# Two attention layers on one core: layer 1's output alternates between two PSUM banks

## The chip, the cores and the metric
The kernel runs on one core of one Trainium2 chip. The metric is the time of one execution on the device in microseconds (us), as the median of a few runs. The core has TensorE (PE in the profile, its weight loads PEld), VectorE (DVE), ScalarE (ACT), GpSimd (POOL) and SyncE (SP), which here only issues DMAs. Each engine works through its own queue in order; semaphores tie them together.

## The reference
The input x is (4, 256, 64, 64) in float32: 4 images of 256 channels and 4096 positions. Two attention layers follow one another.

```
# layer 0, for each image, xf = x as (256, 4096)
q = Wq @ xf + bq;  k = Wk @ xf + bk          # (32, 4096)
v = Wv @ xf + bv                             # (256, 4096)
attn = softmax(q.T @ k, axis=0)              # (4096, 4096), over i
x1   = gamma * (v @ attn) + xf
# layer 1
theta = theta_w @ x1 + theta_b               # (32, 4096)
phi   = maxpool2(phi_w @ x1 + phi_b)         # (32, 1024)
g     = maxpool2(g_w @ x1 + g_b)             # (128, 1024)
attn  = softmax(theta.T @ phi, axis=-1)      # (4096, 1024)
y     = gamma * (out_w @ (g @ attn.T) + out_b) + x1
```

## The kernel before
**Tiles and steps.** The output columns of a layer are cut into 8 chunks of 512 per image, written (l, b, n): layer, image, chunk. The summed dimension is cut into tiles of 128: 32 per chunk in layer 0, 8 in layer 1. One tile is one step g of the program. The chunks run in the order (0,0,0) to (0,0,7), then for each of three images (0,b+1,0), (1,b,0) to (1,b,7), (0,b+1,1) to (0,b+1,7), and last (1,3,0) to (1,3,7). So layer 1 of an image runs between chunk 0 and chunk 1 of the next image's layer 0; for the last image it runs alone, at the end.

**One tile.** PE multiplies keys and queries into one of two banks s_ps (`scores`, L1020), three steps ahead. ACT takes the exponential twice from it, as prob in float32 (L694) and as the rounded prob_h (L697). DVE adds prob to acc, the denominator (L841). POOL forms prob_l = prob - prob_h (`split_prob`, L635), two steps ahead. PE then does `attend`: three matmuls per half of the value channels (L1045 high by high, L1048 high by low, which waits for POOL's prob_l, L1049 low by high) into o_ps. Layer 0 has two halves, ct 0 in o_ps[0] and ct 1 in o_ps[1]; layer 1 has one, always in o_ps[0].

**End of a chunk.** ACT copies o_ps[0] to osb (`copy_o`, L708), in layer 0 DVE copies o_ps[1] (L853). The first attend of the next chunk waits for these copies (L1032, L1034). Jobs D1 (sums, L1091) and D2 (reciprocals spread over the bank, L1095) make the divisor; DVE multiplies osb by it (L927 in layer 0, L936 in layer 1). In layer 0 POOL adds the residual (job N, one per half, L659). In layer 1 PE multiplies by out_w (job Z, one per half, L1099), ACT takes it out of PSUM into zc (L783), and POOL adds x1 (job ZA, L665).

**Jobs beside the tiles.** A plan written out by hand (`make_plan`) gives every other piece of work a step, a place inside the step and a PSUM bank. Place 1 on PE is after the step's scores and ahead of the attends, place 2 between the halves, place 3 behind them. ACT, DVE, POOL and SP run the same jobs in the same order in their own queues, at the end of the step's regular work; DVE runs them ahead of its additions in the last layer-0 chunk of an image and in the last but one step of every chunk. The banks are X0, X1, X2 and A (acc) and, where free, Y = o_ps[1], O0 = o_ps[0], S0, S1 = s_ps. A job waits until the job before it on its bank has been read.

**Maxima.** The softmax is computed with its maximum taken off, which must be known before a chunk's scores. ST jobs (`maxima`, PE L1082, DVE L879) compute 128 queries against 512 keys and reduce them. After the last of a chunk, DVE makes the row of maxima (L885 to L893) and SP writes it into the queries by four DMAs (job M, L591). In layer 1 a chunk has 8 ST: the first four are done earlier, in layer 0, the last four (kc = 1) of chunk n+2 in steps 4 to 7 of chunk n, on Y.

**Projections for the next image.** The last layer-0 chunk of an image, (0,b,7), also computes keys and values of the next image (tables KEYS0 and VALUES0). A K0 job is a projection on PE (six matmuls, L1059 and L1063), whose high part ACT takes (L723) and whose low part DVE takes (K0L, L858); then the bank is free. KEYS0 lists for each: chunk, step and place of K0, bank, step and place of K0L. At step 0 of that chunk D2 stands on X1, where DVE's L927 reads it.

**The last image's entry.** Ahead of (1,3,0) a list of jobs (`before[GATE]`) finishes layer 0 and the maxima of chunk 0; those of chunk 1 are in steps 0 to 3 on X0.

Of the kernel before, what the change touches and what calls it, by code (L numbers as in the profile page):

```python
# [24 lines left out]
B, C, N = 4, 256, 4096  # L25
# [56 lines left out]
def chunk_no(l, b, n):  # L82
    return POSITION[l, b, n]


def chunk_before(l, b, n):
    i = POSITION[l, b, n]
    return SEQ[i - 1] if i else None
# [7 lines left out]
SECOND_BEFORE = {chunk: sum(c[0] for c in SEQ[:i]) for i, chunk in enumerate(SEQ)}  # L96


def summed_in_pairs(l, b, n):
    prev = chunk_before(l, b, n)  # L100
    return l == 0 and (prev is None or prev[0] == 0)
# [24 lines left out]
def begun_at(g, ahead):  # L126
# [3 lines left out]
ROUNDS0 = ((0, 2, (9, 3), (10, 1), (10, 3)), (0, 3, (11, 1), (12, 1), (12, 3)), (0, 4, (15, 3), (16, 1), (16, 3)),  # L130
           (0, 6, (18, 3), (19, 1), (20, 1)), (0, 5, (21, 3), (22, 1), (22, 3)), (0, 7, (22, 3), (23, 1), (23, 3)),
           (2, 6, (26, 3), (27, 1), (27, 3)))
KEYS0 = ((0, (1, 1), X1, (2, 1)), (1, (3, 1), X1, (4, 1)), (2, (12, 1), X1, (13, 1)), (3, (14, 1), X1, (15, 1)),
         (4, (18, 1), X1, (19, 1)), (6, (21, 1), X1, (22, 1)), (5, (23, 3), X1, (24, 3)), (7, (25, 3), X1, (26, 3)))
VALUES0 = ((0, 0, (2, 3), X2, (3, 3)), (0, 1, (4, 3), X2, (5, 3)), (1, 0, (6, 3), X2, (7, 3)),
           (1, 1, (8, 3), X2, (9, 3)), (2, 0, (13, 3), X2, (14, 3)), (2, 1, (15, 1), X2, (16, 1)),
# [11 lines left out]
def make_plan():  # L148
# [3 lines left out]
    def on(job, at):  # L152
        bank[job] = at
        return job

    def maxima(l, b, n, kc, sub, at):
        return on(Job("ST", l, b, n, kc * SUBS + sub), at)
# [10 lines left out]
    def put(g, place, *jobs):  # L168
        for job in jobs:
            during.setdefault(g, []).append(Entry(place, job))  # L170
# [43 lines left out]
    for l, b, n in SEQ:  # L214
        g = tile_no(l, b, n)
        prev = chunk_before(l, b, n)
# [33 lines left out]
        elif not last_of_image:  # L250
# [4 lines left out]
            if more and n >= NCH - 3:  # L255
                i = 2 * (n - (NCH - 3))
# [31 lines left out]
    b, c = B - 1, NCH - 1  # L288
    last = (0, b, c)
    d2 = on(Job("D2", *last, 0), X0)  # L290
    k1, g1 = on(Job("K1", 1, b, c, 0), X0), on(Job("G1", 1, b, c, 0), S0)
    t1 = on(Job("T1", 1, b, c, 0), S0)
    st = [maxima(1, b, 0, 1, s, (X1, Y, S1, X2)[s]) for s in range(SUBS)]
    add = [Job("N", *last, k) for k in range(CT)]
    rnd = rounding(1, b, c)
    k1k, k1q, k1m, k1l = (Job(name, 1, b, c, 0) for name in ("K1K", "K1Q", "K1M", "K1L"))
# [3 lines left out]
    for b in range(B):  # L300
        more = b + 1 < B
        for n in range(NCH):
            g = tile_no(1, b, n)
            if n:
                prev = (1, b, n - 1)
                put(g, 3, on(Job("D2", *prev, 0), X0))
                for k in range(CT):
                    put(g + 2 + 2 * k, 3, on(Job("Z", *prev, k), X0))
                    put(g + 2 + 1 + 2 * k, 3, Job("ZA", *prev, k))
                if n + 1 < NCH:  # L310
                    put(g, 1, Job("M", 1, b, n + 1, 0))
                if n in (4, 5) and not more:
                    for i in range(2):
                        put(g + 5 + i, 1, maxima(1, b, NCH - 1, 0, 2 * (n - 4) + i, X1))
            elif more:
                first = (0, b + 1, 0)
                put(g, 3, on(Job("D2", *first, 0), X0))
                for k in range(CT):
                    put(g + 1 + k, 1, Job("N", *first, k))
                put(g + 1, 1, Job("M", 0, b + 1, 1, 0))  # L320
            else:
                for s in range(SUBS):
                    put(g + s, 3, maxima(1, b, 1, 1, s, X0))
                put(g + 5, 1, Job("M", 1, b, 1, 0))
            put(g + KT[1] - 1, 2, on(Job("D1", 1, b, n, 0), X0))
            if n + 2 < NCH:
                for s, (t, place) in enumerate(((4, 3), (5, 3), (6, 3), (7, 3))):
                    put(g + t, place, maxima(1, b, n + 2, 1, s, Y))

    tail = (1, B - 1, NCH - 1)  # L330
    end = [on(Job("D2", *tail, 0), X0)]
# [73 lines left out]
def build(nc, x_d, w_d, wo_d, cols_d, y_d):  # L405
    f32, f32r = mybir.dt.float32, mybir.dt.float32r
    ALU, ACT, AX = mybir.AluOpType, mybir.ActivationFunctionType, mybir.AxisListType
# [8 lines left out]
    with ctx:  # L416
# [13 lines left out]
        vh = (sb("vh0", [P, KT[0], C], f32r), sb("vh1", [P, KT[1], DV], f32r))  # L430
        vl = (sb("vl0", [P, KT[0], C], f32r), sb("vl1", [P, KT[1], DV], f32r))
# [69 lines left out]
        def image0(b, n):  # L501
            return b * NCH + n
# [20 lines left out]
        def wait_free(eng, job):  # L523
            eng.wait_ge(free[BANK[job]], USE[job] + 1)
# [154 lines left out]
        def _(act):  # L679
# [19 lines left out]
            def copy_o(l, b, n):  # L699

                act.wait_ge(av_done, tile_no(l, b, n, KT[l] - 1) + 1)
                prev = chunk_before(l, b, n)
                if prev is not None:
                    if prev[0] == 0:
                        act.wait_ge(x1_ready, CT * image0(*prev[1:]) + CT)
                    else:
                        wait_scaled(act, *prev)
                nc.scalar.activation(osb[:, 0, :], o_ps[0][:, :], ACT.Copy).then_inc(o_act, 1)  # L708

            def copy_acc(l, b, n):  # L710

# [290 lines left out]
        def _(pe):  # L1002
# [20 lines left out]
            def value(parts, l, t, ct):  # L1023
                return parts[l][:, t, ct * P:(ct + 1) * P]

            def attend(h, ct):
                l, b, n, t = tile_at(h)
                if ct == 0:
                    if t == 0:
                        prev = chunk_before(l, b, n)  # L1030
                        if prev is not None:
                            pe.wait_ge(o_act, chunk_no(l, b, n))  # L1032
                            if prev[0] == 0 and l == 0:
                                pe.wait_ge(o_dve, image0(*prev[1:]) + 1)  # L1034
                        if l == 0 and (prev is None or prev[0] == 1):
                            wait_free(pe, LAST_ON_Y[b])
                        if (h, O0) in LAST_ON:
                            wait_free(pe, LAST_ON[h, O0])
                    if n == 0:
                        wait_free(pe, Job("T1", 1, b, t, 0) if l else Job("V0", 0, b, t // SUBS, t % SUBS // 2))  # L1040
                        if l == 0 and raw(b, t % SUBS // 2):
                            pe.wait_ge(raw_low, t // SUBS + 1)
                    pe.wait_ge(ph_ready, h + 1)
                i, low_at = h % RING, h % PRING
                mm(o_ps[ct][:, :], value(vh, l, t, ct), prob_h[:, i, :], start=t == 0, stop=False)  # L1045
                if ct == 0:
                    pe.wait_ge(pl_ready, h + 1)
                mm(o_ps[ct][:, :], value(vh, l, t, ct), prob_l[:, low_at, :], start=False, stop=False)  # L1048
                last = mm(o_ps[ct][:, :], value(vl, l, t, ct), prob_h[:, i, :], start=False, stop=t == KT[l] - 1)  # L1049
                if ct == VT[l] - 1:  # L1050
                    last.then_inc(av_done, 1)

# [13 lines left out]
            def entry(job):  # L1066
# [2 lines left out]
                name, l, b, c, k = job  # L1069
                at, dst = BANK[job], aux[BANK[job]]  # L1070
                wait(pe, free[at], USE[job])
                if at == Y and (l or b):

                    pe.wait_ge(o_dve, image0(*((b + 1, 0) if b + 1 < B else (b, NCH - 1))) + 1)
                if name == "ST":
                    kc, sub = divmod(k, SUBS)
                    if l:
# [114 lines left out]
```

## Time and profile before

| | us |
|---|---|
| median of 3 runs (2678.57 to 2683.64) | 2683.14 |
| the profiled execution's own time | 2681.38 |
| its span in the profile | 2679.4 |
| PE busy | 2597.6 (97%) |
| PE weight loads busy | 2077.7 (78%) |
| DVE busy | 2015.5 (75%) |
| ACT busy | 1746.0 (65%) |
| POOL busy | 1981.5 (74%) |

Busy times are shares of the whole span. Matmuls overlap in the pipeline: one of 512 columns shows some 0.39 us, but the next can start 0.23 us after it. A single stretch has to be read from the timeline or the windows, where an engine's share can be far from its mean.

### The profile page before, as it was taken

The page shows a single profiled execution, that of the slowest core. Times are in us where ns is not written, and L with a number is a line of the kernel's source. Part 1 is how long each engine was busy: PE and PEld are TensorE (multiplying, and loading weights), DVE is VectorE, ACT ScalarE, POOL GpSimd, SP SyncE. Part 2 cuts the span into 40 slices and gives each one's busy share as a digit, 9 for nine tenths or more (in the row PEclk, how much of TensorE's full clock was granted, in tenths as well). Part 3 has the DMA queues.
Part 4 walks back from the last instruction along what each step waited for, and adds up shares of the span by engine and source line. Part 5 has one row for each costly group of instructions (what it writes and reads, how often), then busy time and mean ns, then how long its engine had stood idle before and what let it go on. Part 6 is the DMA issues. An engine that isn't in the chain of part 4 may idle for free. (4 is left out here: it accounts for less than half of the span.)

```text
span 2679.4 us, 38539 instructions
## 1 busy us (share of the span) xinstructions
PE 2597.6 (97%) x11696; PEld 2077.7 (78%) x11696; DVE 2015.5 (75%) x3352; ACT 1746.0 (65%) x3182; POOL 1981.5 (74%) x1560
## 2 busy tenths in 40 slices
PE   7999999999999999999999999999999999999988
PEld 6788888877778888887777888887777788888756
DVE  6688888777768887876776787887687678877665
ACT  6666666675776666666587666666558766666566
POOL 5677777665897777775699777776569877777668
PEclk9999999999999999999999999999999999999989
DMA  2000000110120000011022000001002100000012
GB/s 91 1 16 17 25 16 20 37 48 17 59 82 26 17 24 17 17 40 40 17 72 79 24 17 16 17 17 47 24 17 88 63 17 16 17 17 16 22 43 71
DMA packets 47656, 88.97 MB, mean 33 GB/s; under 512 B 5344, under 2 KB 5472, under 8 KB 47456
## 3 DMA queue, kind: packets, MB, share of 16 engines
q1 hardware_dynamic: 46896, 85.73, 9.7%
q8 instruction: 99, 1.62, 0.3%
q14 instruction: 101, 0.83, 0.1%
q10 hardware_dynamic: 560, 0.79, 0.1%
HBM read 52.70 MB, written 33.55 MB: 32 GB/s over the span
## 5 line engine op out<-in xcount | busy, mean ns | idle before, releaser
L635 POOL TENSOR_TENSOR prob_l<-prob,prob_h 128x512 fp32r<-128x512 f32 x1280 | 1647.3, 1300 | 650.9 <-PE o_ps L1049 569.7
L694 ACT ACTIVATE prob<-s_ps 128x512 f32<-128x512 f32 x1280 | 767.1, 599 | 771.8 <-PE s_ps L1020 755.2
L879 DVE TENSOR_REDUCE mx<-aux 128x1 f32<-128x512 f32 x1161 | 794.9, 686 | 306.8 <-PE aux L1082 301.7
L1045 PE MATMUL o_ps<-prob_h,vh 128*128 128x512 f32 x2304 | 912.5, 396 | 7.9 <-ACT osb L708 4.9
L1048 PE MATMUL o_ps<-prob_l,vh 128*128 128x512 f32 x2304 | 907.0, 394 | 9.0 <-POOL prob_l L635 7.8
L1049 PE MATMUL o_ps<-prob_h,vl 128*128 128x512 f32 x2304 | 901.4, 391 | 0.0
L841 DVE TENSOR_TENSOR acc<-prob,acc 128x512 f32<-128x512 f32 x1187 | 814.9, 687 | 76.1 <-ACT prob L694 56.5
L697 ACT ACTIVATE prob_h<-s_ps 128x512 fp32r<-128x512 f32 x1280 | 764.9, 598 | 0.0
L1020 PE MATMUL s_ps<-queries,keys 128*128 128x512 f32 x1280 | 523.4, 410 | 23.8 <-DMA queries<-nm_turned 22.7
L1048 PEld LDWEIGHTS o_ps<-prob_l,vh 128*128 128x128 f32 x2304 | 434.5, 189 | 117.7 <-POOL prob_l L635 26.1
L1045 PEld LDWEIGHTS o_ps<-prob_h,vh 128*128 128x128 f32 x2304 | 434.9, 189 | 114.9 <-ACT osb L708 22.2
L1049 PEld LDWEIGHTS o_ps<-prob_h,vl 128*128 128x128 f32 x2304 | 434.2, 188 | 91.2
L1082 PE MATMUL aux<-keys,queries 128*128 128x512 f32 x1161 | 460.0, 396 | 8.3 <-DVE mx L879 3.3
L1020 PEld LDWEIGHTS s_ps<-queries,keys 128*128 128x128 f32 x1280 | 242.3, 190 | 88.6 <-DMA queries<-nm_turned 30.4
L1082 PEld LDWEIGHTS aux<-keys,queries 128*128 128x128 f32 x1161 | 218.4, 188 | 82.5 <-DVE mx L879 16.2
L879 DVE TENSOR_REDUCE mx<-o_ps 128x1 f32<-128x512 f32 x108 | 73.9, 685 | 39.9 <-PE o_ps L1082 39.5
L644 POOL TENSOR_TENSOR xl<-xp,xh 128x512 fp32r<-128x512 f32 x70 | 89.5, 1294 | 5.1 <-ACT xh L738 5.1
L659 POOL TENSOR_TENSOR xa<-osb,xa 128x512 f32<-128x512 f32 x64 | 83.5, 1306 | 9.9 <-DVE osb L927 7.7
L665 POOL TENSOR_TENSOR xa<-zc,xa 128x512 f32<-128x512 f32 x64 | 83.9, 1311 | 6.8 <-ACT zc L783 6.8
L644 POOL TENSOR_TENSOR xl<-xa,xh 128x512 fp32r<-128x512 f32 x64 | 82.1, 1288 | 4.3 <-ACT xh L738 4.3
L912 DVE RECIPROCAL aux<-aux 128x128 f32<-128x128 f32 x88 | 84.3, 958 | 0.0
L723 ACT ACTIVATE queries<-aux,cols 64x512 fp32r<-64x512 f32 x118 | 80.6, 683 | 2.3
(126 smaller groups left out, 1787.2 us busy)
## 6 DMA issues: line engine op xcount, KB each, us to landing
xa<-x SPq DMA_DIRECT2D x32, 512.0 KB, 3.6
xp<-x SPq DMA_DIRECT2D x32, 512.0 KB, 3.6
spill<-xa SPq DMA_DIRECT2D x32, 512.0 KB, 2.8
xa<-spill SPq DMA_DIRECT2D x32, 512.0 KB, 3.6
y<-xa SPq DMA_DIRECT2D x32, 512.0 KB, 2.8
queries<-nm_turned SPq DMA_DIRECT2D x256, 1.0 KB
xp<-spill SPq DMA_DIRECT2D x3, 512.0 KB, 4.6
prob<-w_in ACTq DMA_DIRECT2D x1, 640.0 KB, 5.6
```

The lines of the kernel that those rows point to most:

```text
L635: nc.gpsimd.tensor_tensor(out=prob_l[:, i, :], in0=prob[:, i, :], in1=prob_h[:, h % RING, :].bitcast(f32), op=ALU.subtract).then_inc(pl_re ...
L644: nc.gpsimd.tensor_tensor(out=xl[X_SLOT[r]][:, k, :], in0=src[:, k, :], in1=xh[X_SLOT[r]][:, k, :].bitcast(f32), op=ALU.subtract).then_inc ...
L694: nc.scalar.activation(prob[:, h % PRING, :], s_ps[s][:, :], ACT.Exp).then_inc(p_ready, 1)
L697: nc.scalar.activation(prob_h[:, i, :], s_ps[s][:, :], ACT.Exp).then_inc(ph_ready, 1)
L841: nc.vector.tensor_tensor(out=acc[:, :], in0=prob[:, i, :], in1=acc[:, :], op=ALU.add).then_inc(acc_done, 1)
L879: ins = nc.vector.tensor_reduce(out=dst, in_=bank[:, :], axis=AX.X, op=ALU.max)
L912: nc.vector.reciprocal(bank[:, at], bank[:, at]).then_inc(inverted, 1)
L1020: mm(s_ps[h % SRING][:, :], keys[l][:, key_tile(l, b, t)], queries[:, q_slot(l, b, n), :], start=True, stop=True).then_inc(s_full, 1)
L1045: mm(o_ps[ct][:, :], value(vh, l, t, ct), prob_h[:, i, :], start=t == 0, stop=False)
L1048: mm(o_ps[ct][:, :], value(vh, l, t, ct), prob_l[:, low_at, :], start=False, stop=False)
L1049: last = mm(o_ps[ct][:, :], value(vl, l, t, ct), prob_h[:, i, :], start=False, stop=t == KT[l] - 1)
L1082: last = mm(dst[:, :], queries[:, q_slot(l, b, c), sub * P:(sub + 1) * P], keys[l][:, chunk(kc) if l else key_chunk(b, kc)], start=True, s ...
```

## The change
Layer 1's output goes to o_ps[0] in even chunks and to o_ps[1] in odd ones, and PE's wait for ACT's copy is put where the bank is needed again. Y is no longer free for maxima in layer 1, so these go to X2, at every second step. Job Z of half 1 goes to X1, one step earlier; the second N of chunk (0,b+1,0) goes from step 2 to step 6 (five steps behind the first). Four maxima of the last image go from X1 to X2, one at the last image's entry from Y to O0. In KEYS0 the first projection and its low part are one step later.

```diff
+def output_bank(l, n):
+    return l * n % 2
...
-KEYS0 = ((0, (1, 1), X1, (2, 1)), (1, (3, 1), X1, (4, 1)), ...
+KEYS0 = ((0, (2, 1), X1, (3, 1)), (1, (3, 1), X1, (4, 1)), ...
...
-    st = [maxima(1, b, 0, 1, s, (X1, Y, S1, X2)[s]) for s in range(SUBS)]
+    st = [maxima(1, b, 0, 1, s, (X1, O0, S1, X2)[s]) for s in range(SUBS)]
...
                 for k in range(CT):
-                    put(g + 2 + 2 * k, 3, on(Job("Z", *prev, k), X0))
-                    put(g + 2 + 1 + 2 * k, 3, Job("ZA", *prev, k))
+                    put(g + 2 + k, 3, on(Job("Z", *prev, k), (X0, X1)[k]))
+                    put(g + 3 + 2 * k, 3, Job("ZA", *prev, k))
...
-                        put(g + 5 + i, 1, maxima(1, b, NCH - 1, 0, 2 * (n - 4) + i, X1))
+                        put(g + 5 + i, 1, maxima(1, b, NCH - 1, 0, 2 * (n - 4) + i, X2))
...
-                    put(g + 1 + k, 1, Job("N", *first, k))
+                    put(g + 1 + 5 * k, 1, Job("N", *first, k))
...
-                for s, (t, place) in enumerate(((4, 3), (5, 3), (6, 3), (7, 3))):
-                    put(g + t, place, maxima(1, b, n + 2, 1, s, Y))
+                for s, t in enumerate((1, 3, 5, 7)):
+                    put(g + t, 3, maxima(1, b, n + 2, 1, s, X2))
...
-                nc.scalar.activation(osb[:, 0, :], o_ps[0][:, :], ACT.Copy).then_inc(o_act, 1)
+                nc.scalar.activation(osb[:, 0, :], o_ps[output_bank(l, n)][:, :], ACT.Copy).then_inc(o_act, 1)
...
-                        if prev is not None:
-                            pe.wait_ge(o_act, chunk_no(l, b, n))
-                            if prev[0] == 0 and l == 0:
-                                pe.wait_ge(o_dve, image0(*prev[1:]) + 1)
-                        if l == 0 and (prev is None or prev[0] == 1):
+                        if prev is None:
                             wait_free(pe, LAST_ON_Y[b])
+                        elif l == 0 or n == 0:
+                            pe.wait_ge(o_act, chunk_no(l, b, n) - prev[0])
+                        elif n > 1:
+                            pe.wait_ge(o_act, chunk_no(l, b, n) - 1)
+                        if l == 0 and prev is not None and prev[0] == 0:
+                            pe.wait_ge(o_dve, image0(*prev[1:]) + 1)
+                        if l == 1 and n == 1:
+                            pe.wait_ge(o_dve, image0(*((b + 1, 0) if b + 1 < B else (b, NCH - 1))) + 1)
...
+                elif t == 0 and chunk_before(l, b, n) is not None and chunk_before(l, b, n)[0] == 1:
+                    pe.wait_ge(o_act, chunk_no(l, b, n))
...
-                mm(o_ps[ct][:, :], value(vh, l, t, ct), prob_h[:, i, :], start=t == 0, stop=False)
+                out = o_ps[ct if l == 0 else output_bank(l, n)]
+                mm(out[:, :], value(vh, l, t, ct), prob_h[:, i, :], start=t == 0, stop=False)
...
-                if at == Y and (l or b):
-                    pe.wait_ge(o_dve, image0(*((b + 1, 0) if b + 1 < B else (b, NCH - 1))) + 1)
+                if at == O0 and b > 0:
+                    pe.wait_ge(o_act, chunk_no(0, b, NCH - 1) + 1)
```

## Rows read from the trace of the kernel before

**Rows 1.** The page, part 1: busy us, share of the span, instructions.
```profile
PE 2597.6 (97%) x11696; PEld 2077.7 (78%) x11696; DVE 2015.5 (75%) x3352; ACT 1746.0 (65%) x3182; POOL 1981.5 (74%) x1560
```

**Rows 2.** Windows (PE, PEld, DVE, ACT, POOL busy): layer-0 chunk, layer 1 of images 0, 3.
```profile
128.50:190.30 61.80, 61.80 (x272) 50.39 (x272) 49.47 (x80) 39.55 (x74) 46.25 (x36) 1.00 0.06 18
...
690.00:786.00 96.00, 93.58 (x423) 68.12 (x422) 67.78 (x129) 81.43 (x156) 95.65 (x77) 1.00 0.25 83
...
2584.30:2665.00 80.70, 78.77 (x357) 58.22 (x355) 57.53 (x109) 68.21 (x129) 80.41 (x65) 1.00 0.21 73
```

**Rows 3.** POOL's timeline, layer 1 of image 0: start, us, operation [idle before].
```profile
693.93 8.74 POOL L635 TENSOR_TENSOR prob_l<-prob,prob_h 128x512 fp32r<-128x512 f32 x7
702.86 2.52 POOL L635 TENSOR_TENSOR prob_l<-prob,prob_h 128x512 fp32r<-128x512 f32 x2 [0.19 <-ACT prob_h L697]
...
785.02 5.09 POOL L635 TENSOR_TENSOR prob_l<-prob,prob_h 128x512 fp32r<-128x512 f32 x4
```

**Rows 4.** Weight loads' timeline, first tile after layer 1.
```profile
786.43 0.19 PEld L1048 LDWEIGHTS o_ps<-prob_l,vh 128*128 128x128 f32 x1 [0.36 <-POOL prob_l L635]
```

**Rows 5.** Waits in 690 to 785: us in total, times, longest us.
```profile
PEld o_ps L1048 <- POOL prob_l L635: 6.9, 13, 1.5
...
PEld o_ps L1082 <- DVE mx L879: 3.1, 11, 0.3
...
PEld o_ps L1045 <- ACT osb L708: 1.3, 6, 0.4
```

**Rows 6.** Timelines of PE, ACT and POOL in chunk (1,0,4).
```profile
739.94 1.02 PE L1099 MATMUL aux<-osb,wo 128*128 128x512 f32 x2
...
741.73 0.39 PE L1020 MATMUL s_ps<-queries,keys 128*128 128x512 f32 x1
...
741.08 0.78 ACT L783 ACTIVATE zc<-aux,cb,cols 128x512 f32<-128x512 f32 x1 [0.49 <-PE aux L1099]
...
742.24 0.60 ACT L697 ACTIVATE prob_h<-s_ps 128x512 fp32r<-128x512 f32 x1
...
743.94 2.59 POOL L635 TENSOR_TENSOR prob_l<-prob,prob_h 128x512 fp32r<-128x512 f32 x2
```

**Rows 7.** Timeline of all engines, steps 0 to 3 of chunk (0,0,7).
```profile
507.66 1.41 DVE L927 SCALAR_TENSOR_TENSOR osb<-osb,cols,aux 128x512 f32<-128x512 f32 x2 [2.66 <-PE aux L1095]
507.69 0.40 PE L1020 MATMUL s_ps<-queries,keys 128*128 128x512 f32 x1
...
508.98 0.69 DVE L879 TENSOR_REDUCE mx<-aux 128x1 f32<-128x512 f32 x1
...
509.12 0.50 PE L1059 MATMUL aux<-xh,wh 128*128 128x512 f32 x1 [1.03 <-DVE osb L927]
...
512.40 0.69 DVE L879 TENSOR_REDUCE mx<-aux 128x1 f32<-128x512 f32 x1 [2.13 <-PE aux L1082]
...
513.01 0.69 DVE L841 TENSOR_TENSOR acc<-prob,acc 128x512 f32<-128x512 f32 x1
...
513.73 0.74 DVE L858 SCALAR_TENSOR_TENSOR keys<-aux,cols,keys 32x512 fp32r<-32x512 f32 x1
...
515.22 0.40 PE L1082 MATMUL aux<-keys,queries 128*128 128x512 f32 x1
...
515.65 0.69 DVE L879 TENSOR_REDUCE mx<-aux 128x1 f32<-128x512 f32 x1 [0.42 <-PE aux L1082]
515.69 0.39 PE L1059 MATMUL aux<-xh,wh 128*128 128x512 f32 x1
```

**Rows 8.** Timelines of DVE, PE and POOL, entry of the last image.
```profile
2570.23 0.21 DVE L893 STREAM_TRANSPOSE nm_turned<-nm_cols 128x32 f32<-128x32 f32 x1
...
2574.05 0.80 PE L1020 MATMUL s_ps<-queries,keys 128*128 128x512 f32 x1 [4.02 <-DMA queries<-nm_turned]
...
2575.93 0.63 PE L1082 MATMUL o_ps<-keys,queries 128*128 128x512 f32 x1
...
2584.21 2.53 POOL L635 TENSOR_TENSOR prob_l<-prob,prob_h 128x512 fp32r<-128x512 f32 x2 [0.53 <-ACT prob_h L697]
```

More of the change, by code:

```diff
@@ L132 @@
            (2, 6, (26, 3), (27, 1), (27, 3)))
-KEYS0 = ((0, (1, 1), X1, (2, 1)), (1, (3, 1), X1, (4, 1)), (2, (12, 1), X1, (13, 1)), (3, (14, 1), X1, (15, 1)),
+KEYS0 = ((0, (2, 1), X1, (3, 1)), (1, (3, 1), X1, (4, 1)), (2, (12, 1), X1, (13, 1)), (3, (14, 1), X1, (15, 1)),
          (4, (18, 1), X1, (19, 1)), (6, (21, 1), X1, (22, 1)), (5, (23, 3), X1, (24, 3)), (7, (25, 3), X1, (26, 3)))
@@ L1043, in attend @@
                     pe.wait_ge(ph_ready, h + 1)
+                elif t == 0 and chunk_before(l, b, n) is not None and chunk_before(l, b, n)[0] == 1:
+                    pe.wait_ge(o_act, chunk_no(l, b, n))
                 i, low_at = h % RING, h % PRING
-                mm(o_ps[ct][:, :], value(vh, l, t, ct), prob_h[:, i, :], start=t == 0, stop=False)
+                out = o_ps[ct if l == 0 else output_bank(l, n)]
+                mm(out[:, :], value(vh, l, t, ct), prob_h[:, i, :], start=t == 0, stop=False)
                 if ct == 0:
                     pe.wait_ge(pl_ready, h + 1)
-                mm(o_ps[ct][:, :], value(vh, l, t, ct), prob_l[:, low_at, :], start=False, stop=False)
-                last = mm(o_ps[ct][:, :], value(vl, l, t, ct), prob_h[:, i, :], start=False, stop=t == KT[l] - 1)
+                mm(out[:, :], value(vh, l, t, ct), prob_l[:, low_at, :], start=False, stop=False)
+                last = mm(out[:, :], value(vl, l, t, ct), prob_h[:, i, :], start=False, stop=t == KT[l] - 1)
                 if ct == VT[l] - 1:
```

## The prediction
> **What bounds the kernel now.** I read the page's busy line first: TensorE 97%, GpSimd 74% [rows 1]. The reader should distrust it, because it averages two stages. The windows show them, with the granted clock at 1.00 in all three [rows 2]. In a layer-0 chunk TensorE is busy 61.80 of 61.80 us and its weight loads 50.39 of them (82%), while POOL has 46.25. In 690 to 786 us, which lies inside the layer-1 stretch of image 0, TensorE still shows 93.58 of 96.00, but its weight loads only 68.12 (71%), and POOL 95.65 of 96.00. The last image's layer 1 shows POOL 80.41 of 80.70. So layer 0 runs at TensorE's pace and layer 1 at POOL's.
>
> The Trainium skill (Perfetto Trace Analysis, Identifying the Most-Contended Engine) says the same of the first number: matmul busy time is a bad measure since matmuls are pipelined, and weight-load busy is the better one. The drop from 82% to 71% above agrees.
>
> POOL's own timeline gives its price [rows 3]: seven instructions in 8.74 us, start to start 1.25 us. A layer-1 chunk gives it ten of them (8 prob_l, 2 additions): 12.5 us. From 693.93 to 785.02 + 5.09 = 790.11 it has one gap, 0.19 us before 702.86. The queue is left only when TensorE waits for the first layer-0 tile's prob_l: 0.36 us at 786.43 [rows 4]. That is what sets the end of the stretch; the waits that its weight loads have inside the stretch (3.1 us for maxima, 1.3 us for the copy of the output, against 6.9 us for POOL [rows 5]) are time in which it would otherwise stand before POOL.
>
> **The change, part by part.** Four stretches matter: the layer-1 stretches of images 0 to 2, the last chunk of layer 0 before each of them (three times; the KEYS0 edit), the entry of the last image, and its layer 1.
>
> *Two output banks, in layer 1.* Removed: a wait for ACT's copy at 28 inner boundaries. Z of half 1 goes from step 4 to step 3 and to X1, the maxima from steps 4 to 7 on Y to steps 1, 3, 5, 7 on X2. No instruction is added or taken away on any engine; POOL's order of ten stays. TensorE gets up to 4.4 us per image (3.1 + 1.3 [rows 5]), then stands before POOL. Price for images 0 to 2: 0. The most it can gain is POOL's gap, 0.19 us each. What could lose: the moved Z makes ACT's 0.78 us evacuation stand before the exponentials of tile 7 instead of after them. Before, Z of half 0 is issued at 739.94 and ACT takes it at 741.08, so 1.14 us later [rows 6]. The new Z stands where step 4's scores are (741.73), so ACT takes it at 742.87. The pair of exponentials behind a Z ends 742.24 + 0.60 - 741.08 = 1.76 us after its start, so tile 7 is ready at 744.63. POOL wants it at 743.94 + 1.25 = 745.19: 0.56 us is left. Were ACT 0.86 us later than that, each of 28 chunks would lose 0.3 and the whole 8 us. Upper end +8, lower end -0.5; I take 0, because POOL's gapless row is the nearest one.
>
> *Boundaries.* On entering layer 1 the wait for ACT stays (chunk 0 uses bank 0). On leaving it, half 0 no longer waits for the last copy and half 1 does; but the first tile there waits for POOL, 0.36 us [rows 4], so 0. The second normalizing addition of chunk (0,b+1,0) goes from step 2 to step 6 on POOL: same count before the exit, and its store to spill, the reload of that slot and the next rows of maxima follow it on SP. It then ends about 5 us later (four prob_l of 1.25), which is where the second addition stands in every other layer-1 chunk. ACT's copy of chunk 0's output waits for it, but is due only then. 0.
>
> *KEYS0: the key projection of chunk 0, step 1 to step 2, its low half on DVE, step 2 to step 3.* This is in a TensorE-bound stretch, so it counts in full, three times. All from [rows 7].
> - Gone: the projection waits for X1, held by DVE's two normalizing multiplies (507.66, 1.41 us). It starts at 509.12; scores before it are at 507.69 and the pitch is 0.23, so 1.20 us are idle. A matmul that waited shows 0.50 us, one that did not 0.39: 0.11 more. -1.31.
> - What is late next: step 1's scores for a maximum now come up six matmuls after 507.92, at 509.29, and need X0, which DVE's maximum frees at 508.98 + 0.69 = 509.67. Start 509.72, and 0.11 for the restart: +0.54. Net so far -0.77.
> - New wait: the projection of chunk 1 stays at step 3 on the same X1, and now needs the low half of chunk 0, which has become the first entry of DVE's step 3. In DVE's queue it is behind step 2's maximum, and TensorE issues that one last in step 2. From its issue: 0.43 until DVE starts (515.22 to 515.65), 0.61 maximum, 0.72 addition (513.01 to 513.73), 0.75 and 0.75 for keys and queries, 0.05 to the matmul: 3.31 us. Before, chunk 1's projection follows at 0.47 (515.22 to 515.69). +2.84, and 0.11 for the restart: +2.95. Behind it on TensorE are the attends of step 3, hence all that follows, and POOL and ACT have slack there and can't give it back.
> Net +2.18 per image, +6.5 for three. Bounds: -3.9 (three times the gain, no new wait) and +8.9 (three times 2.95).
>
> *Entry of the last image.* Maxima for chunk 1 (X0, steps 0 to 3) must be done before its scores; these wait for the rows by DMA until 2574.05, 3.6 us after DVE's transpose ends at 2570.44 [rows 8]. DVE sets that pace, and step 1 now has one more maximum on X2: +0.61. Behind the wait a matmul shows 0.63 us instead of 0.39, so each costs some 0.45 instead of the 0.23 pitch, and one maximum less is left to issue there: -0.45. Chunk 1 has one at step 1 instead of later: +0.23. POOL goes gapless only from 2584.21 [rows 8], so this shift moves its whole chain: +0.4 (bounds -1.0 if the freed matmuls pay more, +1.5 with two more DVE slots of 0.61). The scores that go to O0 instead of Y there wait for a copy that is over 10 us old: 0.
>
> **Sum.** 6.5 + 0 + 0.4 = +6.9 us on the profiled execution's 2681.4 us (span 2679.4): 2688.3. The median of the three runs, 2683.1, is 1.8 higher; on it the sum gives 2690.0. I forecast 2689, between the two. Within the case the term bounds give 2684 to 2692.
>
> **Rivals.**
> A. *TensorE's pace sets layer 1 after all.* For: its busy time is 93.58 of 96.00, and it waits for maxima and copies in every chunk. Against: POOL without a gap. It would give back 4.4 us in four images and 0.77 to 1.31 in three: about -17.6 - 3.9 = -21.5, 2660.
> By the Trainium skill (GPSIMD Engine Reference, Elementwise side-by-side cycle accounting) POOL's two-input operation takes some 2.6 cycles an element, which for 512 elements at its 1.2 GHz is an estimate of 1.11 us, 11.1 us a chunk; POOL would then be idle about a tenth of layer 1 and this rival would hold. The trace differs: 1.25 us and no gap, and the measurement decides.
> B. *The new wait on X1 is not there.* DVE reaches the low half before TensorE reaches step 3. Place: DVE's queue at step 2. It needs the maximum of step 2 to be short of 0.47 + 2.84 late, which no row supports. It leaves -0.77 x 3 + 0.4: 2679.5 on the profile, 2680 to 2682 measured; at most -3.9.
> C. *A gap opens in POOL's chain* because the earlier Z keeps ACT from tile 7 (or the later reload keeps the rows of maxima back). It decides once ACT is over 0.6 us later than worked out. +0.3 x 28 = +8 on top of +6.9: 2697.
> The forecast is slower; A and B are the rivals on the other side.
>
> **Chances.** Forecast 0.70, A 0.08, B 0.12, C 0.10. A measurement of this kernel can tell about 0.2%, 5.4 us, from no change. The forecast's +6.9 lies just beyond, so some 0.7 of its 0.70 is slower and the rest no change; C is slower; B is mostly no change, A faster. Faster 0.11, same 0.29, slower 0.60. Range 2677 to 2696: it leaves out A and half of C.
>
> **What would show it.** In the changed profile: (1) a wait of about 2.8 us at L1059 or its weight load for DVE's queries (the low half) near 515 us, and again one image apart (about 659 us), while the 1.5 us wait for the multiplies is gone; (2) POOL 99% busy or more in 690 to 786 plus 2, and the eight layer-1 chunks still about 99 us together; (3) waits for the osb copy gone in layer 1 and waits for prob_l grown by about as much; (4) DVE's transpose about 0.6 us later after the last image's entry. Wrong if POOL shows gaps in layer 1, if the stretch between the copies of (0,1,0) and (1,0,7) falls below 97 us (A), or if step 3's projection does not wait (B).

## The result, and the profile after

The changed kernel takes 2692.2 us (median of 7 runs, 2689.6 to 2694.4), the kernel before 2682.7 (7 runs, 2678.6 to 2683.6): a ratio of 1.0039, with a 95% interval of [1.0029, 1.0049]. That is 9.5 us slower, and inside the predicted 2677 to 2696. The profiled execution, the shortest of the seven, took 2689.6 us, span 2687.5: +8.1 us of span, where the sum said +6.9.

I cut the span at ScalarE's copies of the output, one a chunk, and take from one copy's start to the next. That gives these parts, in us:

| stretch | before | after | difference | predicted |
|---|---|---|---|---|
| (0,0,7), (0,1,7), (0,2,7): last layer-0 chunk of images 0 to 2 | 108.88, 108.37, 108.45 | 112.67, 109.08, 110.69 | +6.7 | +6.5 |
| layer 1 of images 0 to 2 | 98.77 each | 98.57, 98.55, 98.62 | -0.6 | 0 |
| layer 1 of the last image with its entry | 127.05 | 130.55 | +3.5 | +0.4 |
| behind the last copy | 13.0 | 10.9 | -2.1 | 0 |
| all the rest | 1917.3 | 1917.8 | +0.5 | 0 |

The +0.5 lies ahead of the first copy (128.52 and 129.02 us), where the granted clock is 0.95 before and 0.93 after.

**The new wait.** The steps of chunk (0,0,7) that answer to [rows 7], after, from the timelines of PE, DVE and PEld, with the same wait in the next two images:
```profile
510.12 0.50 PE L1094 MATMUL aux<-keys,queries 128*128 128x512 f32 x1 [0.25 <-DVE mx L884]
...
515.30 0.69 DVE L884 TENSOR_REDUCE mx<-aux 128x1 f32<-128x512 f32 x1 [3.34 <-PE aux L1094]
...
518.18 0.23 PEld L1071 LDWEIGHTS aux<-xh,wh 128*128 128x128 f32 x1 [3.12 <-DVE queries L863]
...
518.18 0.74 PE L1071 MATMUL aux<-xh,wh 128*128 128x512 f32 x1 [2.69 <-DVE queries L863]
518.72 0.63 PE L1071 MATMUL aux<-xh,wl 128*128 128x512 f32 x1
519.15 0.63 PE L1071 MATMUL aux<-xh,wh 128*128 128x512 f32 x1
...
1181.55 0.50 PE L1071 MATMUL aux<-xh,wh 128*128 128x512 f32 x1 [2.69 <-DVE queries L863]
...
1841.02 0.50 PE L1071 MATMUL aux<-xh,wh 128*128 128x512 f32 x1 [2.69 <-DVE queries L863]
```
Chunk 1's projection stands 2.69 us for the low half of chunk 0 in every image, and it starts 2.88 us after step 2's maximum starts (515.30 to 518.18). The wait for DVE's multiplies is gone; a small one for the maximum at step 1 is there (0.25).

The three last chunks grow by 3.79, 0.71 and 2.24 us, though the wait is the same. The windows of these steps in images 0, 1 and 2 show where image 0 differs (each row: the window and its length, busy us of PE, PEld, DVE, ACT, POOL with their instructions, the granted clock, and last the DMA share and GB/s):
```profile
504.70:523.00 18.30, 14.76 (x65) 11.67 (x65) 8.74 (x13) 9.25 (x16) 7.63 (x6) 0.91 0.08 30
1168.10:1186.00 17.90, 14.36 (x71) 11.51 (x71) 9.69 (x15) 10.08 (x18) 8.70 (x7) 1.00 0.08 30
1827.60:1846.00 18.40, 14.86 (x73) 11.94 (x73) 10.14 (x16) 10.47 (x18) 8.93 (x7) 1.00 0.08 29
```
Only in image 0 is the clock low behind the wait: a matmul takes 0.63 us, start to start 0.43, which is the 1.2 GHz level, where the others have 0.23. Eight of them lie from 518.18 to 521.70, 3.52 us where eight at 0.23 and the 0.11 of a restart would be 1.95: 1.6 us more. The other images are told by the whole chunks (0,0,7), (0,1,7) and (0,2,7), after:
```profile
504.72:617.39 112.67, 103.24 (x510) 84.17 (x509) 72.40 (x115) 70.13 (x119) 63.32 (x50) 0.97 0.13 38
1168.09:1277.17 109.08, 100.04 (x510) 81.59 (x509) 72.38 (x114) 70.03 (x118) 63.36 (x50) 1.00 0.13 39
1827.56:1938.25 110.69, 101.61 (x510) 83.02 (x509) 72.39 (x114) 70.14 (x118) 63.33 (x50) 0.98 0.11 34
```
Before, the granted clock is 0.98 in all three: each has one spell at 1.2 GHz further on in the chunk, image 1's in 1180 to 1260 us. After, image 0 has two such spells, image 1 none and image 2 one. So image 2 compares like with like, +2.24; image 0 pays 1.6 us more and image 1 some 1.5 us less. The spells are three before and three after, and that is why the mean, +2.25 an image, comes out as the wait's own price; it need not have.

**Layer 1.** After, in answer to [rows 3]: POOL on entering image 0's layer 1.
```profile
694.29 1.30 POOL L664 TENSOR_TENSOR xa<-osb,xa 128x512 f32<-128x512 f32 x1 [0.71 <-PE o_ps L1061]
695.55 6.30 POOL L640 TENSOR_TENSOR prob_l<-prob,prob_h 128x512 fp32r<-128x512 f32 x5
701.78 1.32 POOL L664 TENSOR_TENSOR xa<-osb,xa 128x512 f32<-128x512 f32 x1
703.03 6.29 POOL L640 TENSOR_TENSOR prob_l<-prob,prob_h 128x512 fp32r<-128x512 f32 x5
```
There is no gap from here to 794.07; the 0.19 us gap of before is gone. In answer to [rows 2], a window inside the layer-1 stretch of image 1:
```profile
1354.00:1450.00 96.00, 93.80 (x424) 68.07 (x422) 68.30 (x129) 82.19 (x155) 95.92 (x78) 1.00 0.25 84
```
POOL 95.92 of 96.00, PEld 71%: the same stage with the same bound. And the waits of 694 to 789 (us in total, times, longest), in answer to [rows 5]:
```profile
PEld o_ps L1060 <- POOL prob_l L640: 9.4, 20, 0.8
...
ACT osb L713 <- POOL xa L664: 1.1, 1, 1.1
...
PEld aux L1094 <- DVE mx L884: 0.2, 1, 0.2
```
Waits for maxima fell from 3.1 to 0.2 us, those for the output's copy from 1.3 to nothing (no row), and those for prob_l grew from 6.9 to 9.4. The change did what it says, and the time came back as a wait for POOL.

**The last image.** Its chunks (1,3,4) and (1,3,5) took 13.19 and 12.89 us before and take 14.10 and 14.11 after. The waits of 2624 to 2655, then PE at the end of chunk (1,3,4) and POOL just behind:
```profile
PEld aux L1094 <- DVE mx L884: 4.2, 4, 1.1
```
```profile
2635.15 0.50 PE L1094 MATMUL aux<-keys,queries 128*128 128x512 f32 x1 [0.70 <-DVE mx L884]
2635.48 0.40 PE L1025 MATMUL s_ps<-queries,keys 128*128 128x512 f32 x1
2636.43 0.50 PE L1094 MATMUL aux<-keys,queries 128*128 128x512 f32 x1 [0.55 <-DVE mx L884]
...
2641.12 1.29 POOL L640 TENSOR_TENSOR prob_l<-prob,prob_h 128x512 fp32r<-128x512 f32 x1 [0.43 <-ACT prob_h L702]
2642.94 2.52 POOL L640 TENSOR_TENSOR prob_l<-prob,prob_h 128x512 fp32r<-128x512 f32 x2 [0.53 <-ACT prob_h L702]
```
These two chunks have two more maxima each (of the last chunk's rows). In the changed kernel they are on X2 like all others, so three follow one another on one bank: at place 1 and place 3 of step 5 and at place 1 of step 6. The second waits until DVE has reduced the first (0.70) and stands in front of the next scores; the third waits for the second in turn (0.55) and stands in front of the attends. ACT is late, and POOL gets gaps. Before, these waits were 1.6 us (two), not 4.2 (four).

At the entry, DVE's transpose starts 32.1 us after the last layer-0 copy, before 30.9 [rows 8]; chunks (1,3,0) and (1,3,1) are 0.8 and 0.4 us longer. TensorE stands for the rows of maxima for long here and runs partly at 1.2 GHz. The windows of chunk (1,3,0) before, after and in e1 (below), whose code here is the changed kernel's:
```profile
2539.32:2580.12 40.80, 23.18 (x72) 15.51 (x70) 19.05 (x36) 15.71 (x29) 17.54 (x14) 0.75 0.08 27
```
```profile
2546.00:2587.61 41.61, 23.80 (x71) 16.03 (x70) 19.64 (x37) 15.71 (x30) 17.58 (x14) 0.71 0.08 26
```
```profile
2539.54:2580.27 40.73, 22.89 (x70) 15.30 (x68) 19.75 (x37) 15.72 (x30) 17.58 (x14) 0.75 0.08 26
```
Over all the kernels of this case the chunk's length goes by that clock and not by the code: 40.2 to 40.4 us at 0.79, 40.7 to 41.0 at 0.75, 41.6 to 41.8 at 0.71, 42.3 to 42.7 at 0.68. So the 0.8 us go with the clock. At the same 0.75, (1,3,0) and (1,3,1) take 52.99 before and 53.43 in e1: +0.4, one pair of executions.

**Behind the last copy.** TensorE's last projections, before and then after:
```profile
2670.11 3.75 PE L1099 MATMUL aux<-osb,wo 128*128 128x512 f32 x4 [0.87 <-DVE osb L936]
```
```profile
2679.66 1.95 PE L1111 MATMUL aux<-osb,wo 128*128 128x512 f32 x4 [0.87 <-DVE osb L941]
```
The same four matmuls at the lower and at the higher clock, 1.8 us apart; the eight small ones of D2 ahead of them take 1.76 and 1.13 us. Not all of the 1.8 us is on the path to the end, since ACT takes the first half out while the second is computed; with the 0.6 us of D2 it covers the 2.1. It isn't the edit: e3, whose code here is the changed kernel's, has 3.75 us and a stretch of 13.07.

### The profile page after: what moved, and what is told of

It reads as the page before. It is cut to its first block, busy times and chain, and to the rows that moved or that the text cites. A ratio compares the mean times of both kernels' runs of the same rounds, so it can differ in the third digit from the quotient of the medians.

```text
span 2687.5 us, 38444 instructions
## 1 busy us (share of the span) xinstructions
PE 2598.9 (97%) x11696; PEld 2077.6 (77%) x11696; DVE 2017.0 (75%) x3352; ACT 1748.7 (65%) x3182; POOL 1979.6 (74%) x1560
## 4 chain that ended last, share of the span: by engine, by line
PE 85%; DVE 5%; POOL 4%; issue 3%; ACT 1%; DMA 1%; SPq 0%; POOLq 0%; ACTq 0%; DVEq 0%
PE o_ps L1060 18%; PE o_ps L1057 18%; PE o_ps L1061 18%; PE aux L1094 10%; PE s_ps L1025 10%; PE aux L1071 3%; POOL prob_l L640 3%; PE aux L1128 2%; PE aux L1075 2%; DVE mx L884 1%; PE aux L1111 1%; PE aux L1107 1%; DVE acc L846 1%; POOL xa L670 1%; PE aux L1131 1%
## 5 line engine op out<-in xcount | busy, mean ns | idle before, releaser
L884 DVE TENSOR_REDUCE mx<-aux 128x1 f32<-128x512 f32 x1257 | 860.1, 685 | 357.2 <-PE aux L1094 352.3
L1094 PE MATMUL aux<-keys,queries 128*128 128x512 f32 x1257 | 508.5, 405 | 11.2 <-DVE mx L884 6.4
L1094 PEld LDWEIGHTS aux<-keys,queries 128*128 128x128 f32 x1257 | 236.6, 188 | 95.0 <-DVE mx L884 21.7
L1071 PE MATMUL aux<-xh,wh 128*128 128x512 f32 x180 | 72.9, 405 | 13.5 <-DVE queries L863 8.1
```

Source lines behind the costliest of these rows:

```text
L884: ins = nc.vector.tensor_reduce(out=dst, in_=bank[:, :], axis=AX.X, op=ALU.max)
L1071: mm(dst, w[:, kt, w0:w0 + width], xh[X_SLOT[r]][:, kt, :], start=first, stop=False)
L1094: last = mm(dst[:, :], queries[:, q_slot(l, b, c), sub * P:(sub + 1) * P], keys[l][:, chunk(kc) if l else key_chunk(b, kc)], start=True, s ...
```

## The experiments

Each ran in 5 rounds beside the kernel before; the ratios are to that series. "L1 stretch" is layer 1 of one of images 0 to 2, copy to copy.

### e1_keys_back and e2_keys_only: the KEYS0 edit taken out, and alone

The edit of e1, against the changed kernel; e2 is the kernel before with the new tuple, nothing else changed:
```diff
-KEYS0 = ((0, (2, 1), X1, (3, 1)), ...
+KEYS0 = ((0, (1, 1), X1, (2, 1)), ...
```


> The changed kernel with the KEYS0 edit undone (projection of chunk 0 at step 1, its low half at step 2). Theory (the edit costs 2.2 us an image by a new wait on X1; what is left of the change costs 3.4 us in the last image and gives back 0.2 in each other layer-1 stretch): 2.9 us over the kernel before, some 2685.5, and the 2.7 us idle of TensorE before chunk 1's projection is gone. Rival (the loss is in the layer-1 rearrangement or in the clock, and the wait on X1 only replaces other waiting): it stays 8 us or more over the kernel before, 2691 or more.

> The kernel before with the KEYS0 edit alone. Theory: three times 2.2 = 6.5 us slower, some 2689, with a wait of 3.1 us of the weight load for DVE's low half in each of three images. Rival (the wait costs nothing by itself): within 1.5 us of the kernel before. A third reading: the wait also lets the granted clock fall now and then, which adds some 1.2 us an image to it: 2690 to 2692.

Measured: e1 2681.8 us, ratio 1.0002 [0.9993, 1.0011]; e2 2690.2 us, 1.0032 [1.0021, 1.0043]. The chunks (0,b,7) are 108.89, 108.47 and 108.51 in e1 and 112.70, 109.09 and 110.80 in e2, against 108.9, 108.4, 108.5 before and 112.7, 109.1, 110.7 after. One tuple of two steps is the whole measurable loss, and the other edits cost nothing on the median (2.9 us had been expected).

e2's own cost is less sure than its cause: its chunks add up to +6.9 us, its medians differ by 8.6 (2690.2 less 2681.6, interval 5.6 to 11.5). That fits the theory (6.5) and as well the third reading, in which the clock adds to the wait; nothing here tells the two apart.

### e3_low_half_early: the same, with the low half a step sooner

```diff
-KEYS0 = ((0, (2, 1), X1, (3, 1)), ...
+KEYS0 = ((0, (2, 1), X1, (2, 1)), ...
```


> The changed kernel with the low half of chunk 0's keys taken in DVE's step 2, ahead of that step's maximum; the projection stays at step 2. Theory (the cost is the low half's place in DVE's queue, not the projection's step): chunk 1's projection waits some 0.5 us instead of 2.7, three times 2.3 us less than the changed kernel, 2685. Rival (two projections one step apart are too close for ACT and DVE in any order): no gain over the changed kernel, 2692.

Measured: 2680.9 us (2685 expected), 0.9998 [0.9989, 1.0006]; the chunks (0,b,7) take 108.11, 106.18 and 107.72, a mean of 107.3 where before has 108.6 and after 110.8. No wait for queries is left at the projections, whose six matmuls follow the scores at the pitch; the first two:
```profile
514.69 0.40 PE L1025 MATMUL s_ps<-queries,keys 128*128 128x512 f32 x1
514.93 0.39 PE L1071 MATMUL aux<-xh,wh 128*128 128x512 f32 x1
515.16 0.40 PE L1071 MATMUL aux<-xh,wl 128*128 128x512 f32 x1
```
So the wait was the position of the low half in DVE's queue, as step "new wait" of the prediction has it, and the net -0.77 us of its first two terms is there too: -0.77 in image 0 and -0.73 in image 2, where the granted clock is 0.98 as before. Image 1 has -2.19, but its clock is 1.00 where before has 0.98, worth 1.5 us as above.

### e4_last_maxima_apart and e5_layer1_alone: two maxima on one bank kept apart

The edit of e4, on the changed kernel; e5 is e4 with KEYS0 of the kernel before:
```diff
-                        put(g + 5 + i, 1, maxima(1, b, NCH - 1, 0, 2 * (n - 4) + i, X2))
+                        put(g + 4 + 2 * i, 3, maxima(1, b, NCH - 1, 0, 2 * (n - 4) + i, X2))
```


> The changed kernel with the four maxima of the last image's chunk 7 at place 3 of steps 4 and 6 instead of place 1 of steps 5 and 6, so that no two jobs follow one another on X2 inside a step. Theory (TensorE waits 4.2 us of weight loads for X2 in chunks 4 and 5, and POOL's chain has gaps of 2.5 us there): 2 us less than the changed kernel, 2690, and POOL's gaps in these chunks gone. Rival (POOL's rate sets that stretch anyway): no difference, 2692.

> The changed kernel with the KEYS0 edit undone and the last image's four maxima at steps 4 and 6, place 3: what is left is the two banks and the moved jobs of layer 1. Theory (POOL's ten operations of 1.25 us set a layer-1 chunk): stretches of 98.6 us in images 0 to 2 against 98.8, and 1 us less in the last image than before: 2680.5, within 0.1% of the kernel before. Rival (TensorE's pace sets layer 1 and the last image's loss hid the gain): 10 us or more faster, 2671 or less.

Measured: e4 2690.3 us, 1.0031 [1.0020, 1.0042]; e5 2679.1, 0.9991 [0.9983, 1.0000]. Chunks (1,3,4) and (1,3,5) fall from 14.10 and 14.11 to 12.72 and 12.65 (e5: 12.71, 12.65), below before's 13.19 and 12.89. The waits of e4 in 2620 to 2650 are more in number and short:
```profile
PEld aux L1094 <- DVE mx L884: 1.7, 6, 0.3
```
That is 2.8 us of chunk time, read off the copies; it is 0.1% of the whole, and the medians (2692.2, 2690.3) can't confirm it. e5 is layer 1 of the change without its mishap: L1 stretches 98.6, 0.9 us less in layer 1 over all four images, and the 2 us of clock at the very end. It is the theory's result (2680.5, within 0.1%), and the rival, 10 us or more faster, is out.

### e6_before_add_on_dve and e7_layer1_add_on_dve: one of POOL's ten instructions moved to DVE

e6 is on the kernel before, e7 on e5; the first hunk is POOL's loop, the second DVE's:
```diff
-                elif name == "ZA":
+                elif name == "ZA" and k == 0:
...
+                elif name == "ZA" and k == 1:
...
+                    nc.vector.tensor_tensor(out=xa[slot][:, k, :], in0=zc[:, k, :], in1=xa[slot][:, k, :],
+                                            op=ALU.add).then_inc(y_ready, 1)
```


> The kernel before with the second addition of each layer-1 chunk (ZA of half 1) on DVE instead of POOL: nine POOL operations a chunk, 11.25 us. Theory: TensorE's own pace on one output bank, 12.1 us, becomes the bound in chunks 0 to 5 and POOL's 11.25 in 6 and 7: some 3 us less per image, 2669. Rival 1 (POOL was not the bound): no difference, 2682. Rival 2 (an addition from two SBUF inputs on DVE and POOL's operations keep each other out, so POOL's slot is paid anyway): 2678 or more, and POOL's prob_l or DVE's addition show times well over 1.30 and 0.70 us.

> The same move of the second addition to DVE, in the kernel of e5 (two output banks). Theory (the two banks give TensorE a pace of 11.0 to 11.3 us a chunk, hidden before by POOL's 12.5): chunks of 11.3 us, 8 us less per image, 2650: the two banks are worth 15 to 20 us more here than nothing in e5. Rival (the two banks give TensorE nothing): the same as the kernel before with this move, 2669. If DVE and POOL keep each other out, both are less: 2665 and a chunk near 12 us.

Measured: e6 2703.2 us, 1.0081 [1.0068, 1.0093], L1 stretches 103 to 106; e7 2687.1, 1.0022 [1.0013, 1.0030], stretches 100.2 to 101.2. Both theories missed: both kernels are slower than the kernel before. What came is the sign that rival 2 of e6 names, an addition well over 0.70 us. The groups of that one line by its shape (busy us, mean ns of one), in e6 and e7:
```profile
L982 DVE TENSOR_TENSOR xa<-zc,xa 128x512 f32<-128x512 f32 x32 | 42.7, 1333 | 8.6 <-ACT zc L784 4.9 <-POOL xa L666 3.7
```
```profile
L987 DVE TENSOR_TENSOR xa<-zc,xa 128x512 f32<-128x512 f32 x32 | 56.2, 1757 | 4.9 <-ACT zc L789 4.9
```
An addition that I had counted at some 0.7 us took 1.33 and 1.76 on the mean. It takes 0.69 with POOL idle; beside POOL mostly 1.36 to 1.39 or 1.85 in e6 and 1.52 or 1.8 in e7, and in e7 once in each of images 0 to 2 some 5.95. That one in image 0, on DVE and POOL:
```profile
707.44 5.94 DVE L987 TENSOR_TENSOR xa<-zc,xa 128x512 f32<-128x512 f32 x1
713.30 0.68 DVE L885 TENSOR_REDUCE mx<-aux 128x1 f32<-128x512 f32 x1
...
706.58 6.24 POOL L640 TENSOR_TENSOR prob_l<-prob,prob_h 128x512 fp32r<-128x512 f32 x5
716.68 1.26 POOL L640 TENSOR_TENSOR prob_l<-prob,prob_h 128x512 fp32r<-128x512 f32 x1 [3.86 <-PE o_ps L1069]
```
The addition starts while POOL is in the first of five prob_l and ends 0.56 us after the last (706.58 + 6.24 = 712.82). Then the maximum behind it comes 5 us late, TensorE waits 3.4 us for its bank, ACT 4.2 for scores, POOL 3.9 for a slot: chunk (1,0,2) takes 18 us, and so do (1,1,2) and (1,2,2). In the steady chunks (11.3 to 11.9 us) the lighter POOL does pay, but POOL is slowed too. Its eight prob_l in a row take 10.63 us, where six took 7.5 (1.25 each), so DVE's addition costs it 0.6 us a chunk:
```profile
734.62 1.30 POOL L671 TENSOR_TENSOR xa<-zc,xa 128x512 f32<-128x512 f32 x1
735.88 10.63 POOL L640 TENSOR_TENSOR prob_l<-prob,prob_h 128x512 fp32r<-128x512 f32 x8
```
These nine follow one another without a gap and give the 11.9 us of these chunks. In e6 the same addition of 1.36 us at 744.77 makes a maximum late in the steady chunks (13.3 us), and TensorE, whose maxima of steps 4 to 7 share the bank Y, waits for it:
```profile
746.79 0.19 PEld L1090 LDWEIGHTS o_ps<-keys,queries 128*128 128x128 f32 x1 [1.48 <-DVE mx L880]
```
The Trainium skill (SBUF — State Buffer, SBUF: two separate sides) says that of a VectorE instruction with two SBUF inputs and a GpSimd one that reads SBUF, whichever starts first has the shared pair of ports for the whole instruction, and the other is blocked. The trace agrees in kind and is harder: here VectorE's addition ended only behind five GpSimd instructions in a row, 5.94 us after its start.

### e8_all_mended: e3 and e4 together, and the last entry's maxima late

```diff
-                for s, t in enumerate((1, 3, 5, 7)):
+                for s, t in enumerate((1, 3, 5, 7) if n or more else (4, 5, 6, 7)):
```


> The changed kernel with the low half of chunk 0's keys in DVE's step 2, the last image's four maxima apart, and at its entry the maxima of chunk 2 in steps 4 to 7 instead of 1, 3, 5, 7. Theory (the costs add up): last layer-0 chunks 3.7 us less than before in three images together, layer 1 0.2 less in each, the last image 1.5 less: 2677. Rival (what is saved at one place is waited for at the next): 2681 or more.

Measured: 2677.3 us, 0.9984 [0.9976, 0.9993], chunks (0,b,7) 106.54, 107.74, 107.72, L1 stretches 98.6, (1,3,4) and (1,3,5) 12.68 and 12.64. Faster than both kernels by a little, and the theory's 2677. But its terms did not all come: the last image with its entry took 128.20 us, 1.2 more than before and not 1.5 less, and the last stretch behind the copy is 2.1 us shorter by the clock, which no term had. The edit of the entry showed nothing: chunk (1,3,0) took 41.81 us against after's 41.61, both at a granted clock of 0.71.

### e9_no_pool_add: POOL's additions gone, with two output banks

On e8. DVE gets the new instruction, straight from PSUM; POOL's additions and ACT's evacuations, two each a chunk, go, and the scale moves into the weights once at the start:
```diff
+                elif name == "Z":
...
+                    nc.vector.scalar_tensor_tensor(
+                        out=xa[slot][:, k, :], in0=bank[:, :], scalar=cb[:, k:k + 1], in1=xa[slot][:, k, :],
+                        op0=ALU.add, op1=ALU.add).then_inc(free[BANK[job]], 1)
...
-                    nc.gpsimd.tensor_tensor(out=xa[slot][:, k, :], in0=zc[:, k, :], in1=xa[slot][:, k, :],
-                                            op=ALU.add).then_inc(y_ready, 1)
...
-                    nc.scalar.activation(zc[:, k, :], bank[:, :], ACT.Identity, bias=cb[:, k:k + 1],
-                                         scale=cols[:, COL_G1:COL_G1 + 1]).then_inc(free[BANK[job]], 1)
...
+            nc.vector.tensor_scalar(wo[:, :], wo[:, :], cols[:, COL_G1:COL_G1 + 1], None, ALU.mult)
```


> The kernel of e8, but in layer 1 DVE takes Z out of PSUM and adds the bias and x1 in one operation (out_w is scaled by gamma once at the start), so that ACT's two evacuations and POOL's two additions of each chunk are gone. POOL has eight operations a chunk, 10.0 us, DVE some 10.8, ACT 9. Theory: TensorE becomes the bound of layer 1 at some 10.9 us a chunk with maxima and 10.3 without, 12 us less per image: 2630. Rival (DVE becomes the bound, or its order delays the exponentials): chunks stay at 11.5 us or more, 2650.

Measured: 2652.7 us (4 runs), 0.9900 [0.9884, 0.9917], L1 stretches 92.89, 92.63 and 93.29, steady chunks 11.74 and the last two of an image, which have no maxima, 10.9. The times are the rival's (2650, 11.5 or more), the bound is the theory's: TensorE is busy 90.00 of 90 us and DVE 73.61 (below), so what the theory had wrong is TensorE's pace, by 0.6 to 0.8 us a chunk. The new instruction reads one input from PSUM and one from SBUF, and does not run into POOL (742 to 752 ns over all 64):
```profile
L971 DVE SCALAR_TENSOR_TENSOR xa<-aux,cb,xa 128x512 f32<-128x512 f32 x64 | 48.0, 750 | 23.9 <-PE aux L1104 23.7
```

### e10_one_bank_no_pool_add: the same with one output bank

e9's edit and e3's KEYS0 on the kernel before. What sets it apart from e9 (-) is that layer 1 has one output bank and its maxima on Y at steps 4 to 7 (+):
```diff
-                out = o_ps[ct if l == 0 else output_bank(l, n)]
...
-                for s, t in enumerate((1, 3, 5, 7) if n or more else (4, 5, 6, 7)):
-                    put(g + t, 3, maxima(1, b, n + 2, 1, s, X2))
+                for s, (t, place) in enumerate(((4, 3), (5, 3), (6, 3), (7, 3))):
+                    put(g + t, place, maxima(1, b, n + 2, 1, s, Y))
```


> e9_no_pool_add without the change's second output bank: the kernel before (one output bank in layer 1, maxima and additions placed as there), with chunk 1's low half a place before its projection as in e3_low_half_early, and layer 1's second addition made on DVE straight out of PSUM (GpSimd's two additions and ScalarE's two evacuations a chunk gone). It tells what the second bank is worth once GpSimd no longer sets the pace. Theory: TensorE's pace now sets layer 1, and a chunk's first attend must wait for the copy of the last output again; in the kernel before such waits are 0.2 to 1 us a chunk, some 0.5 us, on 28 chunks = 14 us, so about 2667 us, the layer-1 stretches near 97 us in place of e9's 92.9. Rival: the four maxima in one bank at four steps running cost as much as the copy, up to 1.1 us each as in the last image of the changed kernel: 4 us a chunk, stretches over 98 us, about 2680 us, no better than before. Rival: the score matmul and the maxima issued ahead cover the wait, and it runs in e9's time, 2653 us, so that the second bank is worth nothing.

Measured: 2678.4 us, 0.9987 [0.9978, 0.9996], L1 stretches 99.22, 99.26, 99.22, steady chunks 12.59. Windows of layer 1, e9 and then e10, and e10's waits in 700 to 790:
```profile
700.00:790.00 90.00, 90.00 (x422) 70.34 (x421) 73.61 (x135) 69.86 (x135) 77.38 (x62) 1.00 0.28 95
```
```profile
700.00:790.00 90.00, 87.20 (x403) 65.69 (x402) 70.44 (x130) 66.32 (x129) 73.15 (x59) 1.00 0.26 89
```
```profile
PEld o_ps L1075 <- DVE mx L865: 5.4, 10, 0.8
...
PEld o_ps L1038 <- ACT osb L703: 1.7, 2, 1.1
```
POOL has 77 and 73 of 90 us, so it bounds neither. In e10 TensorE's weight loads wait 5.4 us for maxima and 1.7 for the output's copy in these 7.2 chunks, about 1.0 a chunk; e9 has no row of either kind there, and its chunk is 0.85 us shorter. The theory had only the copy and 97 us a stretch; the first rival (maxima in one bank at four steps running) names the larger part and the stretch.

The two waits take turns. Chunks 6 and 7 have no maxima, and there e10 is slower than e9 by as much (12.00 and 11.91 us against 10.92 and 10.85), with one wait for the copy in place of those for maxima:
```profile
773.48 0.19 PEld L1038 LDWEIGHTS o_ps<-prob_h,vh 128*128 128x128 f32 x1 [1.09 <-ACT osb L703]
```
So the single output bank costs about 1 us a chunk by itself. One bank with the maxima spread over X2 was not run; by these chunks I would expect the copy's wait to take the place of the other.

Four kernels, one question: the mean L1 stretch, and the median less that of before in the same series. The three new ones share e3's KEYS0, whose own gain is some 2 us (3 times 0.75); the clock makes it 2.0 to 3.8 us of chunk time.

| | POOL adds twice a chunk | POOL adds nothing |
|---|---|---|
| one output bank | 98.8 (before) | 99.2 (e10, -4) |
| two output banks | 98.6 (e8, -5) | 92.9 (e9, -27) |

The second column also relieves ACT of two evacuations a chunk, and no run parts the two. ACT was busy 81.43 of 96.00 us where POOL had no gap [rows 2, 3].

## Why the prediction was right, and where it was off

- *POOL bounds layer 1, so two banks are worth 0*: right. 98.77 to 98.6 us, which is the gap of 0.19 us that the prediction gave as the most to gain, POOL without a gap, and what TensorE no longer waits for maxima and copies it waits for prob_l. With POOL's (and ACT's) load away the same edits give 6.3 us a stretch (e10 to e9). That the first column of the table is flat and the second isn't is the proof; e10 shows the converse, that this relief is worth nothing either on one bank.
- *ACT's slack for tile 7 (0.56 us; rival C)*: right in images 0 to 2, no gap on POOL. In the last image POOL has gaps (up to 0.74 us), by another way; there the prediction's own sign of being wrong, gaps on POOL in layer 1, is met.
- *KEYS0, +2.18 an image*: right, +2.24 in image 2, where the clock is alike, +2.25 on the mean, +2.30 in e2. The new wait is where it was put and goes when the low half is moved (e3). Its three terms: the wait for the multiplies is gone; step 1's wait for the maximum shows 0.25 us idle (0.43 by the prediction's rows); the projection starts 3.31 us after step 2's maximum is issued (514.87 to 518.18), as worked out. The first two terms by themselves are e3: -0.77 and -0.73. That the three images differ by 3 us was not foreseen: I had no term for the clock, and that its spells are as many before as after was luck. The medians of e2 leave room for a cost of up to 11.5 us in place of 6.5.
- *Entry of the last image, +0.4*: the profile shows +1.2, inside the bound of 1.5, but 0.8 of it goes with the granted clock of chunk (1,3,0), 0.71 against 0.75. At an equal clock e1 gives +0.4. DVE's transpose is later by 1.1 to 1.2 us, not by 0.6, and most of that is given back behind it.
- *Layer 1 of the last image, 0*: wrong, the failed step. "The maxima from steps 4 to 7 on Y to steps 1, 3, 5, 7 on X2" was worked out for seven chunks in eight alike; in chunks 4 and 5 of the last image the maxima of the last chunk's rows come on top and change from X1 to X2, and I gave that line no term. The two chunks measured +2.1 us, and lose 2.8 when the maxima are kept apart (e4). The total came out in the range in spite of it.
- *The sum*: +6.9 against +8.1 of span: +0.2 from KEYS0, -0.6 from layer 1, +3.1 from the last image (3.5 less the 0.4: 2.1 by the step that failed, 0.8 by the clock, 0.2 in other chunks), -2.1 behind the last copy by the clock, +0.5 ahead of the first copy, where the clock is lower too. The misses nearly cancel, and the closeness of the total owes something to that. By the medians the change costs 9.5 us, 2.6 more than the sum.
- *Rival B* fell with the wait itself, *rival A* with POOL's rows. A's mechanism is real one bound further on: e9's 11.74 us a chunk is what TensorE, without a gap, gives once POOL has eight instructions and there are two banks.
- My expectations for e6 and e7 failed on one price: DVE's addition of two SBUF operands against a POOL that never pauses.

## What to carry to other kernels

Where one engine runs without a gap, relief for the others is worth nothing alone, and relief for that engine may be worth nothing alone either, if a second bound stands right behind it (12.46 us by POOL, 12.59 by the banks): try the two together before dropping either. When a job moves to a bank or a step, list every job on that bank in the order of issue, the rare ones of the last iteration too, and for each the place in its consumer's queue that frees the bank. An instruction moved to an idle engine should be priced beside what will run next to it.

## What the hardware showed that I had not expected

- A VectorE addition with two SBUF inputs, 0.69 us alone, took 1.33 and 1.76 us on the mean and 5.95 us at worst beside GpSimd. In that worst case GpSimd kept its own pace (five in 6.24 us); else it paid as well, 0.4 us a chunk in e6 (a group of four takes 5.46 in place of 5.0 us) and 0.6 in e7. With one input from PSUM the operation took 0.75 us every time.
- The same 2.69 us wait of TensorE left the clock at 2.4 GHz in two images and was followed by 3.5 us at 1.2 GHz in the third; and the last four projections ran at either level in kernels whose code there is the same (3.75 and 1.95 us). Two executions have to be compared at equal granted clock, stretch by stretch, before 1 or 2 us in a stretch are read as an edit's worth: in the last layer-0 chunks one more spell is 1.5 us, and at the last image's entry a clock of 0.71 in place of 0.75 is 0.8.
